# First attention with a growing value lag, a five to three split of its last products, and three layer normalisations batch by batch

## The reference, cut to what matters

```
x = x + cross(layernorm(x), ctx)      # stage 1
x = x + relative(layernorm(x))        # stage 2, self attention with relative positions
x = x + routed(layernorm(x))          # stage 3, self attention, then gates over heads, projection
layernorm(x) = (x - mean) / sqrt(var + 1e-5)
cross: q = y Wq + bq; k = ctx Wk + bk; v = ctx Wv + bv
       a = softmax(q k^T / sqrt(32)) over HEADS AND BATCH PAIRS (axis 0), not over keys
       out = (a v) Wo + bo
```

## Time and profile before

| what | value |
|---|---|
| median of 3 runs (lowest, highest) | 936.7 us (935.32, 937.66) |
| profiled execution, its own time | 937.31 us |
| its span | 935.5 us |
| mean granted PE clock | 0.933 of full speed |
| PE busy | 797.7 us, 85% of the span |
| DVE busy | 634.5 us, 68% |
| ACT busy | 487.0 us, 52% |
| POOL busy | 478.0 us, 51% |
| chain that ended last, by engine | PE 72%, DVE 9%, ACT 6%, SP's queue 4%, DMA 4%, issue 3%, POOL 1% |
| mean of one POOL product L870 (one piece) | 2151 ns |
| mean of one POOL value bias L842 | 1295 ns |
| mean of one POOL low part of a weight L853 | 4625 ns |
| mean of one ACT exponential L644 | 1063 ns |

### The profile page before, as it was taken

One profiled execution on the slowest core, in us unless ns is written; L12 is line 12 of the kernel. 1 busy time (PEld: TensorE's weight loads), 2 busy tenths in 40 slices (PEclk: granted clock), 3 DMA queues, 4 the chain that ended last, 5 costly groups with the idle time before them and its releaser, 6 DMA issues.

```text
span 935.5 us, 14835 instructions
## 1 busy us (share of the span) xinstructions
PE 797.7 (85%) x6274; PEld 594.7 (64%) x6274; DVE 634.5 (68%) x519; ACT 487.0 (52%) x653; POOL 478.0 (51%) x256
## 2 busy tenths in 40 slices
PE   5889999999999999999999999868785132839878
PEld 2556777777777777777777777646665132727557
DVE  5048888788887887887887888895330009384895
ACT  4348557567476476475575675643321038523261
POOL 0026876876877867867868768595310111112200
PEclk9979999999999999999999999988887666959999
DMA  7110110110110110100101101011489850001001
GB/s 269 42 45 4 43 46 2 46 47 1 46 46 2 46 46 1 46 23 24 47 1 46 46 1 46 1 46 47 189 229 261 189 142 1 21 26 46 1 1 46
DMA packets 30353, 52.71 MB, mean 56 GB/s; under 512 B 2384, under 2 KB 25296, under 8 KB 26576
## 3 DMA queue, kind: packets, MB, share of 16 engines
q1 hardware_dynamic: 30288, 51.77, 18.3%
HBM read 41.87 MB, written 9.90 MB: 55 GB/s over the span
## 4 chain that ended last, share of the span: by engine, by line
PE 72%; DVE 9%; ACT 6%; SPq 4%; DMA 4%; issue 3%; POOL 1%; ACTq 0%; DVEq 0%
PE ps L299 22%; PE ps L307 21%; PE ps L352 13%; PE ps L370 6%; SPq L190 4%; DMA rel_scratch<-blocks 3%; PE ps L315 3%; PE ps L381 1%; PE ps L290 1%; ACT s_buf L749 1%; PE ps L502 1%; ACT v_buf L627 1%; DVE blocks L1087 1%; DVE s_buf L1186 1%; DVE rmax L1184 1%
## 5 line engine op out<-in xcount | busy, mean ns | idle before, releaser
L870 POOL TENSOR_TENSOR s_buf<-s_buf,r_all 128x1024 f32<-128x1024 f32 x94 | 198.7, 2151 | 2.9 <-DVE r_all L1025 2.9
L635 ACT COPY s_buf<-ps 128x1024 f32<-128x1024 f32 x128 | 129.7, 1013 | 68.3 <-PE ps L352 68.3
L352 PE MATMUL ps<-q_blk,k_t 64*128 64x256 f32 x1024 | 147.7, 408 | 6.7 <-ACT s_buf L635 6.7
L983 DVE TENSOR_REDUCE extra<-s_buf 128x128 f32<-128x2048 f32 x48 | 109.4, 2280 | 42.3 <-ACT s_buf L635 42.3
L644 ACT ACTIVATE s_buf<-s_buf 128x1024 f32<-128x1024 f32 x128 | 135.7, 1063 | 4.6 <-DVE s_buf L1005 4.5
L352 PEld LDWEIGHTS ps<-q_blk,k_t 64*128 64x128 f32 x1024 | 89.3, 188 | 54.8 <-issue 38.6
L619 ACT ACTIVATE k_t<-ps,cols 128x512 f32<-128x512 f32 x64 | 44.0, 688 | 129.6 <-PE ps L299 129.6
L1005 DVE TENSOR_TENSOR s_buf<-s_buf,ps 128x2048 f32<-128x2048 f32 x48 | 106.9, 2283 | 0.5
L1012 DVE TENSOR_REDUCE ps<-s_buf 128x128 f32<-128x4096 f32 x16 | 70.8, 4428 | 45.3 <-ACT s_buf L644 45.3
L848 POOL TENSOR_TENSOR odd_lo<-raw,odd_hi 128x512 fp32r<-128x512 f32 x32 | 41.3, 1290 | 113.8 <-ACT odd_hi L612 113.8
L842 POOL TENSOR_TENSOR v_buf<-v_buf,extra 128x512 f32<-128x512 f32 x64 | 82.7, 1295 | 14.6 <-ACT v_buf L627 14.6
(11 more groups left out here) (178 smaller groups left out, 1384.2 us busy)
## 6 DMA issues: line engine op xcount, KB each, us to landing
raw<-in_ctxT SPq DMA_DIRECT2D x16, 1024.0 KB, 4.8
s_buf<-rel_scratch SPq DMA_DIRECT2D x64, 128.0 KB, 4.0
rel_scratch<-blocks SPq DMA_DIRECT2D x10, 810.0 KB, 7.7
raw<-in_Wk SPq DMA_DIRECT2D x2, 1024.0 KB, 5.4
raw<-in_Wq SPq DMA_DIRECT2D x2, 1024.0 KB, 6.1
raw<-in_Wv SPq DMA_DIRECT2D x2, 1024.0 KB, 4.9
extra<-in_EvRel SPq DMA_DIRECT2D x1, 2048.0 KB, 9.5
x_res<-in_x SPq DMA_DIRECT2D x1, 1024.0 KB, 5.5
```

The source lines that it names most:

```text
L352: last = mm(ps[:, 2 + half_rows, i * 2 * P:(i + 1) * 2 * P], k_t[rows, hg, b * P:(b + 1) * P], q_blk[rows, b * C + hg, :], start=True, sto ...
L635: copy(piece(t, p).rearrange("p e (u n) -> p (e u) n", u=2), ps[:, 2:4, :]).then_inc(s["s_evac"], 1)
L870: pool.tensor_tensor(part, part, spread(r_all, 4), ALU.mult).then_inc(s["attn_pool"], 1)
L983: nc.vector.tensor_reduce(m_ps if k == 0 else m_next[:, k % 2, :], over_pairs(t, 2 * k, 2), AX.XY, ALU.max).then_inc(s["max_done"], 1)
```

## The change

Four edits. **(1)** Values get their steps from a list: in the order of tiles and batches they take steps 4, 5, 6, 7, 12, 14, 20, 21, 22, 23, 28, 29, 31, 36, 37, 39, then 44 to 47 and so on as before, up to 124 to 127 for tile 14 and 129 to 132 for tile 15 (before: 132 to 135). So steps 4 to 7, empty of a projection before, get one; steps 13, 15, 30 and 38 lose theirs. The same list sets the copies on ACT. **(2)** In the last tile DVE multiplies five pieces (two, two, one), POOL three, and POOL's low part of Wo comes behind the four value biases. **(3)** The normalisations go batch by batch: statistics, root (eps is the bias of the root), reciprocal, y, four transposes into one bank, copy and low part per batch. **(4)** After the first attention its output goes to `odd_hi`, `odd_lo` instead of `x_hi`, `x_lo`, so that the transposes of the first two batches, and what follows them, can stand among the output projections (first two batches behind the third and fourth projection); the keys of the second attention wait for the high parts at the start and for the low parts only at their last third; and ACT's softplus (Exp, Ln) stands ahead of these copies.

```diff
+        FREE = (13, 15, 30, 38, 128)
+        v_cycles = [n for n in range(8 * T + 5) if (n % 8 >= 4 or n >= 8 * T) and n not in FREE]
+        k_cycles = [n for n in range(8 * T) if n % 8 < 4]
+        cycles = sorted(k_cycles + v_cycles)
+
         def k_step(t, i):
-            return i if t == 0 else 8 * t - 4 + i
+            return cycles.index(k_cycles[C * t + i])
 
         def v_step(t, b):
-            return min(8 * t + 8, 8 * T - 4) + b
+            return cycles.index(v_cycles[B * t + b])
+
+        def v_at(n):
+            return divmod(v_cycles.index(n), B) if n in v_cycles else None
 
         def dve_pieces(t):
-            return 2 if t < T - 1 else 4
+            return 2 if t < T - 1 else 5
...
-            def transposes(y, banks, k):
-
+            def transposes(y, k, b):
+
+                pe.wait_ge(s["ln_done"], B * k + b + 1)
                 for c in range(C):
-                    for b in range(B):
-                        if c == 0:
-                            pe.wait_ge(s["ln_done"], B * k + b + 1)
-                        last = nc.tensor.transpose(ps[:, banks + c, b * P:(b + 1) * P], y[:, b, c * P:(c + 1) * P], ident[:])
-                    last.then_inc(s["tr_done"], 1)
+                    last = nc.tensor.transpose(ps[:, 4 + b, c * P:(c + 1) * P], y[:, b, c * P:(c + 1) * P], ident[:])
+                last.then_inc(s["tr_done"], 1)
...
                     if n == 2 and low_ready is not None:
-                        pe.wait_ge(s["ctx_lo"], low_ready)
+                        pe.wait_ge(s[low_ready[0]], low_ready[1])
...
-            def out_proj(slot, bank, done, b):
+            def out_proj(slot, bank, done, b, x_parts=x_parts):
...
-            transposes(y_ln0, 4, 0)
+            for b in range(B):
+                transposes(y_ln0, 0, b)
...
-                if i >= 4 and 1 <= t <= T:
-                    project_v(t - 1, i - 4)
+                if v_at(n):
+                    project_v(*v_at(n))
...
             for b in range(B):
                 pe.wait_ge(s["x_lo_done"], b + 1)
-                out_proj(0, b, s["wo_psum"], b)
-
-
-            transposes(y_ln, 4, 1)
+                out_proj(0, b, s["wo_psum"], b, x_parts=ctx_parts[1])
+                if b >= 2:
+                    transposes(y_ln, 1, b - 2)
+            for b in range(2, B):
+                transposes(y_ln, 1, b)
             weight_ready(1)
-            pe.wait_ge(s["x_lo_done"], 2 * C)
+            pe.wait_ge(s["x_hi_done"], 3 * C)
             for hg in range(C):
                 pe.wait_ge(s["x1_done"], hg + 1)
-                proj_t(1, hg, s["k2_psum"], hg)
+                proj_t(1, hg, s["k2_psum"], hg, low_ready=("x_lo_done", 2 * C))
...
-            transposes(y_ln, 4, 2)
+            for b in range(B):
+                transposes(y_ln, 2, b)
...
-            def ln_std(k):
-                act.wait_ge(s["var_done"], k + 1)
-                nc.scalar.activation(rstd[:], rstd[:], ACT.Sqrt).then_inc(s["std_done"], 1)
+            def ln_std(k, b):
+                act.wait_ge(s["mv_done"], B * k + b + 1)
+                nc.scalar.activation(rstd[:, b:b + 1], mean_var[:, b, 1:2], ACT.Sqrt, bias=eps).then_inc(s["std_done"], 1)
...
-            ln_std(0)
-            for c in range(C):
-                act.wait_ge(s["tr_done"], c + 1)
-                copy(x_t0[:, c, :], ps[:, 4 + c, :]).then_inc(s["x_hi_done"], 1)
+            act.wait_ge(s["eps_done"], 1)
+            for b in range(B):
+                ln_std(0, b)
+            for b in range(B):
+                act.wait_ge(s["tr_done"], b + 1)
+                copy(x_t0[:, :, b * P:(b + 1) * P],
+                     ps[:, 4 + b, :].rearrange("p (c q) -> p c q", c=C)).then_inc(s["x_hi_done"], 1)
...
-                if i >= 4 and 1 <= t <= T:
-                    v_copy(t - 1, i - 4)
+                if v_at(n):
+                    v_copy(*v_at(n))
...
+            def split_hi(k, b):
+                act.wait_ge(s["tr_done"], B * k + b + 1)
+                if k == 1:
+                    act.wait_ge(s["kv_psum"], 8 * T)
+                copy(x_hi[:, :, b * P:(b + 1) * P],
+                     ps[:, 4 + b, :].rearrange("p (c q) -> p c q", c=C)).then_inc(s["x_hi_done"], 1)
+
 
             act.wait_ge(s["soft_a"], 1)
             nc.scalar.activation(soft[:, 1], soft[:, 0], ACT.Exp).then_inc(s["soft_b"], 1)
             act.wait_ge(s["soft_b"], 1)
             nc.scalar.activation(soft[:, 2], soft[:, 1], ACT.Ln, bias=1.0).then_inc(s["soft_c"], 1)
 
-            ln_std(1)
-            for c in range(C):
-                act.wait_ge(s["tr_done"], C + c + 1)
-                split_hi(c, 4 + c)
+
+            for b in range(B):
+                act.wait_ge(s["av_done"], 8 * (T - 1) + 4 + b + 1)
+                copy(odd_hi[:, b, :], ps[:, 4 + b, :]).then_inc(s["x_hi_done"], 1)
+            weight_hi(1)
+            for b in range(B):
+                ln_std(1, b)
+                if b >= 2:
+                    split_hi(1, b - 2)
+            for b in range(B - 2, B):
+                split_hi(1, b)
...
-            ln_std(2)
-            for c in range(C):
-                act.wait_ge(s["tr_done"], 2 * C + c + 1)
-                split_hi(c, 4 + c)
+            for b in range(B):
+                ln_std(2, b)
+                if b >= 2:
+                    split_hi(2, b - 2)
+            for b in range(B - 2, B):
+                split_hi(2, b)
...
             for t in range(T):
                 subtract(t)
+                between(t)
                 if t == T - 1:
                     weight_lo(0)
-                between(t)
                 normalise(t)
...
-            def layer_norm(k, ready):
-                for b in range(B):
-                    ready(b)
-                    nc.vector.bn_stats(stats[:, b, :], x_res[:, b, :]).then_inc(s["stats_done"], 1)
-                for b in range(B):
-                    dve.wait_ge(s["stats_done"], B * k + b + 1)
-                    nc.vector.bn_aggr(mean_var[:, b, :], stats[:, b, :]).then_inc(s["mv_done"], 1)
-                dve.wait_ge(s["mv_done"], B * (k + 1))
-                nc.vector.tensor_scalar(rstd[:], mean_var[:, :, 1], EPS, None, ALU.add).then_inc(s["var_done"], 1)
-                dve.wait_ge(s["std_done"], k + 1)
-                nc.vector.reciprocal(rstd[:], rstd[:]).then_inc(s["rstd_done"], 1)
-                dve.wait_ge(s["rstd_done"], k + 1)
-                for b in range(B):
-                    y = y_ln0 if k == 0 else y_ln
-                    nc.vector.tensor_scalar(y[:, b, :], x_res[:, b, :], mean_var[:, b, 0:1], rstd[:, b:b + 1],
-                                            ALU.subtract, ALU.mult).then_inc(s["ln_done"], 1)
+            def moments(k, b):
+                nc.vector.bn_stats(stats[:, b, :], x_res[:, b, :]).then_inc(s["stats_done"], 1)
+                dve.wait_ge(s["stats_done"], B * k + b + 1)
+                nc.vector.bn_aggr(mean_var[:, b, :], stats[:, b, :]).then_inc(s["mv_done"], 1)
+
+            def normalised(k, b):
+                y = y_ln0 if k == 0 else y_ln
+                dve.wait_ge(s["std_done"], B * k + b + 1)
+                nc.vector.reciprocal(rstd[:, b:b + 1], rstd[:, b:b + 1]).then_inc(s["rstd_done"], 1)
+                dve.wait_ge(s["rstd_done"], B * k + b + 1)
+                nc.vector.tensor_scalar(y[:, b, :], x_res[:, b, :], mean_var[:, b, 0:1], rstd[:, b:b + 1],
+                                        ALU.subtract, ALU.mult).then_inc(s["ln_done"], 1)
+
+            def split_lo(k, b):
+                dve.wait_ge(s["x_hi_done"], B * (k + 1) + b + 1)
+                cols_b = slice(b * P, (b + 1) * P)
+                tt(x_lo[:, :, cols_b], ps[:, 4 + b, :].rearrange("p (c q) -> p c q", c=C), x_hi[:, :, cols_b],
+                   ALU.subtract).then_inc(s["x_lo_done"], 1)
 
             for j in range(J):
                 rows = slice(j * HD, (j + 1) * HD)
                 nc.vector.memset(q_mul[rows, j % 2:j % 2 + 1], SCALE).then_inc(s["qmul_done"], 1)
                 nc.vector.memset(q_mul[rows, 1 - j % 2:2 - j % 2], 0.0).then_inc(s["qmul_done"], 1)
             dve.wait_ge(s["x_in"], 16)
-            layer_norm(0, lambda b: None)
+            nc.vector.memset(eps, EPS).then_inc(s["eps_done"], 1)
+            for b in range(B):
+                moments(0, b)
+                if b >= 1:
+                    normalised(0, b - 1)
+            normalised(0, B - 1)
...
             def normalise(t):
                 dve.wait_ge(s["r_psum"], t + 1)
-                for u in range(dve_pieces(t) // 2):
-                    part = pairs(t, 2 * u, 2)
-                    tt(part, part, r_wide.broadcast_to([P, 8, P, 2]), ALU.mult).then_inc(s["attn_dve"], 1)
+                for p in range(0, dve_pieces(t), 2):
+                    n = min(2, dve_pieces(t) - p)
+                    part = pairs(t, p, n)
+                    tt(part, part, r_wide.broadcast_to([P, 4 * n, P, 2]), ALU.mult).then_inc(s["attn_dve"], 1)
...
```

(31 more changed lines are left out.)

13 lines of the change are left out of this document (3 added, 10 removed).

## The result

The changed kernel takes **941.27 us** (median of 6 runs, 938.85 to 942.42), the kernel before 936.62 beside it (6 runs, 935.32 to 937.66): a ratio of 1.0045, 95% interval 1.0029 to 1.006. It is slower, by 4.6 us, where 4.6 us of gain were forecast. The profiled execution is its quickest, 938.85 us by itself, 1.5 above the profiled one of before; the other 3 us lie between executions, and the experiments had to find them.

What follows compares the result with a forecast made beforehand. PE was taken to bound full tiles (busy 36.08 of 36.20 us), with waits elsewhere. Loop -3.3, tail +0.8, normalisations -0.7, -2.1 and +0.7 summed to -4.6 us: median 932.1 from 936.7, range 928.5 to 936.5.

Steps and rivals of the forecast that it cites:

- values in steps 4 to 7: Early first attention: filling four score-only steps with V projections delays the start of step 9 by 3.6 us.
- steps 13, 15: Steps emptied of a projection where ACT is busy too: -1.0 us for both, bounds 0 and -2.95 x 2.
- steps 30, 38: Emptied steps with a burst of products: the whole projection goes, -2.95 us each, -5.9 together; bounds 0 and -5.9.
- tail: End of the first attention: exponentials wait behind the third V's copy, +0.8 us; bounds -3.4 and +3.
- first normalisation, start: Four transposes left at the end instead of 16, so the projection behind starts 0.7 us earlier.
- query projection: Behind the first normalisation: starts earlier by that stretch's gain, with no change of its own length costed.
- second normalisation: Second attention's keys start 17.9 us behind the output projection's start instead of 20.06: -2.1 us.
- third, start: Third normalisation, nothing lying over it: queries start at 843.7 instead of 843.08, +0.7 us rounded up.
- rival D: Softmax chain, not PE, sets the pace at steps 34 and 42: 938.0 or 939.0 us, chance 0.11.
- five to three split: Tail's last products, five pieces on DVE and three on POOL: worth about 0.8 us of the tail.
- A: The forecast itself: 932.1 us, own range 930.5 to 933.8, chance 0.55.
- B: Third attention's queries start slow behind spread transposes: +1.6 us, so 933.7; chance 0.16.

Runs made afterwards that it cites:

- f3: Changed kernel plus unread transposes of the identity in PE's idle time, 40 ahead of the first normalisation's transposes, 35 around the third's: 936.78 us (0.9999).
- h5: h2 with the wait for the root's constant moved from ACT to DVE: 939.98 us (1.0021 to the kernel before).
- f1: Kernel before with only the second normalisation batch by batch: 937.16 us (0.9999).
- f4: Kernel before with the second normalisation, the five to three split and a value list leaving steps 4 and 5 empty instead of 13 and 15: 931.74 us (0.9943).
- h2: Changed kernel with the root's constant written before DVE's wait for x: 939.81 us (1.0028 to the kernel before).
- e2: Changed kernel with the first normalisation as before: 939.71 us (1.0021 to the kernel before).
- e3: Kernel before with only the new list of value steps, last products split four to four: 936.45 us (1.0001).
- h1: Changed kernel with the third normalisation as before: 937.88 us (1.0001 to the kernel before).
- e4: Kernel before with only the third normalisation batch by batch: 940.01 us (1.003).
- h6: g3 with the first normalisation by batch as in h5: 929.27 us (0.9896 to the kernel before).
- g4: Kernel before plus 40 idle transposes at the start and five in each of steps 4 to 7: 935.65 us (0.9969).
- g3: f4 plus 40 idle transposes at the start, last two V projections in steps 133, 134, five transposes each in steps 4, 5, eleven in the second normalisation: 924.59 us (0.9867).
- h4: g3 run again unchanged for a second profile: 926.99 us (0.9878 to the kernel before).
- h3: g3 without the eleven idle transposes in the gaps of the second normalisation: 929.37 us (0.9909 to the kernel before).

## Why the prediction was wrong

The terms, against the pair of profiles and against the means over the profiles of the table (with the part less without it; f3 left out where it fills, h5 for the start):

| term | forecast | the two profiles | means |
|---|---|---|---|
| values in steps 4 to 7 | +3.6 | +3.4 | +4.8 |
| steps 13, 15 | -1.0 | +0.3 | +0.6 |
| steps 30, 38 | -5.9 | -5.9 | -5.9 |
| tail | +0.8 | +0.5 | +1.4 |
| first normalisation, start | -0.7 | 0.0 | 0.0 |
| query projection | 0 | +2.7 | +1.8 |
| second normalisation | -2.1 | -2.7 | -2.5 |
| third, start | +0.7 | +0.6 | +0.6 |
| third's queries | 0 | +1.9 | +2.1 |

(Query projection without the change: 14.52 in five profiles, 16.44 in f1, 16.55 in f4.) The means give +2.9 for the sum, the measurement +4.6 (+2.7 to +5.6); h2 and h5, with the same schedule but for the constant and its wait, measured +2.6 and +2.0. Part of the difference lies in the runs beside it: the six of the kernel before have a median of 936.6, all 139 on record 937.35, and the changed kernel with h2 940.4 over 18, which would be +3.1. In the pair of profiles the terms give +0.8 of 1.6; the other 0.8 lie in the second attention (187.41 against 185.97 us from its keys to the third's queries, of which the table has 0.6), and the spread of that stretch named above is not explained.

- **Right.** Steps 30 and 38: -5.9 to a tenth; the slack of 4.7 us at POOL held, and rival D is out. The mechanism of the tail: exponentials behind the third V's copy (forecast 613.0, seen 613.32), DVE's products at 629.6 (629.87); the changed kernel was 0.4 late on this clock before the tail. DVE's chain from the first sum took 10.82 us where the forecast had 10.9, with 2 us in it that no row carried. Its size was 0.5 in the pair and 1.4 in the mean, forecast 0.8; that spread is the pace of PE's last 96 matmuls (3.31 to 3.59 us in the three tails of 61.35 to 61.61, 4.69 to 4.88 in the five of 62.51 to 62.70). The five to three split, 0.8 of it in the forecast, showed nothing (e2 against e3). The second normalisation: 17.9 us forecast, 17.38 seen. The start of the third: 13.3 forecast, 13.27 seen.
- **Wrong: "the projection behind it starts earlier by that, its operands being loaded already".** This step costed only when PE may start, not how fast it then runs. Behind spread transposes the query projection ran at half speed for its first matmuls, in all five profiles with the changed first normalisation and no fill: 2.7 us in three, 2.4 and 1.5 in the others. Behind one piece it did so in two of seven (f1, f4). And the 0.7 itself was lost to the table load, which the sum had left at its old place though the change put a second wait ahead of it.
- **Wrong: the choice of A over B.** The forecast named the slow start of the third's queries and gave it 0.16, with the argument that they had been quick after idling before. But what differed before was that the 16 transposes ran in one piece. The rule of the Trainium skill named there ("TensorE: Matmul & The Clock Gate", section "HAM oscillation — how this bites in real kernels") is borne out here by h1 against e4 (1.19 and 2.07 us). The price was mis-sized a little too: 1.6 in the forecast, 1.9 in the pair. And a rule that holds at one place of the kernel had to be asked at all: it was applied to the third normalisation and not to the first, where the same edit was made.
- **Mis-sized: "-1.0 for the two" steps 13 and 15.** ACT sets the pace there; emptying PE turned the gain into waits of 2.67 and 1.99 us and a slow start of step 16. With +0.6 in the mean, its bound of 0 was too kind as well.
- **Mis-sized: +3.6 for steps 4 to 7.** Correct for the execution read, but 11.4 us for four steps are 9.0 at full speed. The half speed seen in three scores was taken for a fixed cost of that stretch.
- **Off, without weight in the sum.** Three products on POOL from 629.6 on end at 636.0, not 635.7 (635.91 seen). And x + bo ended at 640.91 before, not 640.4: the first residual, at 640.94, waited for it.

## What to carry to other kernels

When work is split to start the next matmuls earlier, cost what PE does just before them: ahead of the third's queries sixteen transposes in one piece beat four times four with gaps. Where the next matmuls start slow either way, as the second's keys do, splitting has little to lose (the stretch is 2.5 us shorter). Price a stretch that shows half-speed matmuls twice, as seen and at full speed, before calling its time the kernel's. Empty a step of PE only where PE is what the step waits for, and order the in-order engine's stream by the end of the chain: moving two V copies behind the exponentials gave about 2 us.

## Unexpected of the hardware

- The query projection lost 2.7 us (17.21 against 14.52) with a granted clock of 1.00 in both windows. So early in the span the clock record missed what the matmuls show. In h6, whose idle transposes come first, the same slow start stands beside a granted clock of 0.54. Windows of h6 (columns as in the earlier trace rows):

```profile
14.76:18.76 4.00, 4.00 (x5) 1.76 (x6) 3.00 (x5) 4.00 (x6) 0.00 (x0) 0.54 0.87 345
```

- The table load for the root stands ahead of a single wait on ACT (0.73) but behind two (7.45), and 7.47 with the constant already there.
- Idle transposes that cost PE time made the whole quicker: f3 is 4.5 us quicker than the changed kernel, g4 2.0 us quicker than the kernel before (935.65 against 937.66), g3 and h4 together 3.6 us quicker than h3.
